# A decoder kernel: the first iteration of fp8 attention placed beside the last two state space iterations

## The chip, the cores and the metric

The kernel runs on one core of a Trainium2 chip. The metric is the device time of one execution in microseconds (us), the median of several runs. The core has five engines with a queue each, worked off in order: TensorE (PE) multiplies matrices, VectorE (DVE) and ScalarE (ACT) do elementwise work, GpSimd (POOL) does a share of it, and SyncE (SP) issues the DMAs. Engines wait for each other through semaphores. Matmul results land in PSUM, which has eight banks; all other data lies in SBUF.

## The reference

Six layers run one after another over 16 sequences of 128 tokens with 256 channels, each followed by a residual sum and a layer norm: linear attention, cross attention, a ternary MLP, a state space layer, fp8 attention, and a ternary linear layer. The change touches the fourth and the fifth. Cut to what matters:

```python
# layer 4: state space (per sequence)
zxbcdt = x @ W_in.T
xBC = silu(causal_conv(xBC, conv_w))
dt = softplus(dt_raw + dt_bias)
M = CB * Lmat * dtc[:, :, None, :, :]
Yd = jnp.einsum('bcijh,bcjhp->bcihp', M, xs_c)
yz = (Yd + D * xs) * silu(z)
return (yz * rsqrt(mean(yz * yz) + EPS) * norm_w) @ W_out.T

# layer 5: fp8 attention, self and cross, 32 query heads and 8 key/value heads each
ln_out = _ln(hidden_states, ln_w, ln_b)
q = _ln(_fp8_linear_pertensor(ln_out, wq, ...)); k, v, qx likewise
core = _gqa(q, k, v)
kx, vx = jnp.split(jnp.einsum('bsi,oi->bso', cond, w_kv_x), 2, axis=-1)
xout = _gqa(qx, _ln(kx, ...), vx)
catq = _div_clamp_fp8(jnp.concatenate([core, xout], axis=-1), proj_smooth)
return jnp.einsum('bsi,oi->bso', catq, wproj) * (proj_in_scale * proj_w_scale)
```

## The kernel before

One sequence (128 tokens on the 128 partitions) is one iteration of every stage. The stages follow each other; in each, the five engines have their own list of instructions, written out by hand in a function per engine (`sync`, `gpsimd`, `tensor`, `scalar`, `vector`), and the lists are worked off in order. A stage is pipelined in software: `steps(m, side, attend, front, back, ...)` is one iteration's worth of an engine's list, in which `front` prepares sequence m + 1, `attend` works on sequence m and `back` ends sequence m - 1.

**State space** (`state_space`, from line 1156). `sequences` calls `steps` for m = 0 to 17. In `attend`, the decay matrix is worked off in seven levels: TensorE multiplies `cb` and `xd` of a level into one of two banks `pL` (line 1404), VectorE scales the result by `dec` into `term` (1618), and GpSimd adds `term` to `y` (1350). Of the next sequence, `front` makes the projections and convolutions (banks `pZ`, `pX`, `pC`, `pE`), `xdt` and `xd`. In `back`, `y` is gated by `sz` (1625), transposed (1424), multiplied with `w_out` (1433), summed with `X` (1664) and normed; `vector_apply` (112) writes it back to `X`. m = 16 has `attend` and `back`, m = 17 only `back`. Beside this, m = 0 to 14 prepare the fp8 weights in `fa.w_all`.

**fp8 attention** (`fp8_attention_and_linear`, from line 1693). Each `steps` has eight units j = 0 to 7, one per four query heads. In `front`, unit j makes one block of four heads of keys or values of the next sequence, in the order k0, k1, v0, v1, k2, k3, v2, v3 (`OTHERS`; k0, k1, v0, v1 from the context `ctxT`, line 1910; the others from the quantised input, 1890). A key or query block is projected by TensorE into `pJB` or `pJA`, squared by ScalarE (2031), its `rs` made by GpSimd (1843, 1846), scaled by VectorE (`kn` 2174, `qn` 2180), transposed by TensorE into `pH` (1973, 2012) and copied by ScalarE (`kT`, `qT`, 2038); value blocks are only copied (`v`, 2076). The input is normed (`xn`, 2130), transposed (1999), copied (`lnT`, 2067) and quantised into four streams `xq` by VectorE and GpSimd (`stream_input`, 2139 to 2150; 1866; 2230). The first iteration, m = 0, has only `front`: units 0 to 7, and with them units 5 to 7 start queries 0 to 2 of sequence 1 (`there(j + 3)` and so on). Text calls it the head.

**Projection weights.** In the head SyncE loads `fa_wproj` in eight pieces of 512 KB into two buffers `wp_raw`, which lie in `cat`; a piece c from the third on waits until piece c - 2 is done (`wp_low`). ScalarE copies a piece to bf16 (2080, counted by `wp_high`), VectorE subtracts the copy (2234, counted by `wp_low`); both lie in `w_proj`, in the region shared with weights of the state space stage. Unit j treats piece j.

**The handover.** Every engine's list of the attention stage begins with `left` of the state space stage: a wait until `X` of the last sequence is written (`norm.x_done`), then one for `fa_ready`. After it come the iterations m = 0, 1, 2, 3, a hardware loop, and the last three. The eight PSUM banks of both stages are the same ones in turn, and their SBUF tensors overlap.

## Time and profile before

| | us |
|---|---|
| median of 3 runs | 2179.44 (2178.09 to 2184.95) |
| profiled execution | 2178.37 |
| its span, first to last instruction | 2176.6 |
| busy of the span: PE, DVE, ACT, POOL | 2028.2, 1624.8, 1333.5, 1274.6 |
| mean granted TensorE clock | 0.982 |

The span is what the profile shows from the first to the last instruction. The granted clock is the share of TensorE's full rate that the chip allowed: 1.00 is 2.4 GHz, 0.50 is 1.2 GHz. The state space stage ends at 1276.6 us of the span, where `X` of the last sequence is written; the head of the attention stage reaches to some 1330 us.

### The profile page before, as it was taken

How to read it: one execution, taken by the hardware profiler on the slowest of the kernel's cores; microseconds unless marked ns; L12 is line 12 of the kernel's file. 1: busy time of each engine (PE TensorE's matmuls, PEld its weight loads, DVE VectorE, ACT ScalarE, POOL GpSimd, SP SyncE). 2: the span in 40 equal slices, each digit the busy share in tenths (PEclk: the TensorE clock that was granted, in tenths of full speed). 3: DMA queues.
4: the chain of work that ended last, by engine and by line, in shares of the span. 5: the costliest groups of instructions: out<-in, count | busy, mean ns of one | idle time of the engine just before them, and what ended most of it. 6: DMA issues, size and time to landing. Idle time of an engine off the chain costs nothing.

```text
span 2176.6 us, 35701 instructions
## 1 busy us (share of the span) xinstructions
PE 2028.2 (93%) x10116; PEld 1329.1 (61%) x10116; DVE 1624.8 (75%) x3833; ACT 1333.5 (61%) x5022; POOL 1274.6 (59%) x1550
## 2 busy tenths in 40 slices
PE   7879999999999998899999957999999999999995
PEld 5636666666666665555655524666666666666664
DVE  7845667677776777787888746788888888788886
ACT  3555666666666665333343326777777777777773
POOL 0154454455444542578876734777777777777774
PEclk9999999999999999999999979999999999999998
DMA  6000000000000003000000011000000000000000
GB/s 225 1 18 6 3 4 3 2 5 2 2 2 2 2 1 141 9 20 20 20 20 10 1 47 40 4 4 6 6 6 5 6 5 6 8 5 6 3 3 8
DMA packets 30094, 37.62 MB, mean 17 GB/s; under 512 B 3328, under 2 KB 24320, under 8 KB 29312
## 3 DMA queue, kind: packets, MB, share of 16 engines
q1 hardware_dynamic: 29952, 36.11, 5.0%
q8 instruction: 42, 0.69, 0.1%
q14 instruction: 100, 0.82, 0.1%
HBM read 34.00 MB, written 2.10 MB: 17 GB/s over the span
## 4 chain that ended last, share of the span: by engine, by line
PE 63%; DVE 15%; ACT 11%; issue 7%; POOL 3%; DMA 0%; DVEq 0%; SPq 0%; POOLq 0%; ACTq 0%
PE xa_pS L755 5%; PE xa_pJB L736 5%; PE xa_pO L830 5%; PE xa_pY L867 5%; PE fa_pJB L1910 5%; PE xa_pJA L736 4%; PE ssm_pX L1410 4%; PE fa_pS L1929 3%; PE fa_pY L1962 3%; PE fa_pO L1949 3%; PE fa_pJA L1890 2%; PE ssm_pL L1404 2%; PE fa_pH L2012 2%; PE xa_pP L747 2%; POOL fa_rs L1846 2%
## 5 line engine op out<-in xcount | busy, mean ns | idle before, releaser
L2038 ACT ACTIVATE fa_qT<-fa_pH,all_fa_head_vec 128x512 f32<-128x512 f32 x128 | 99.6, 778 | 177.9 <-PE fa_pH L2012 177.9
L1846 POOL TENSOR_TENSOR fa_rs<-fa_rs,all_minus_half 128x4 f32<-128x4 f32 x192 | 197.9, 1031 | 15.0
L1350 POOL TENSOR_TENSOR ssm_y<-ssm_y,ssm_term 128x512 f32<-128x512 f32 x112 | 142.2, 1270 | 81.5 <-DVE ssm_term L1618 57.1
L2047 ACT ACTIVATE fa_pS<-fa_pS,fa_nb 128x128 f32<-128x128 f32 x512 | 183.3, 394 | 6.0 <-issue 6.0
L1843 POOL TENSOR_TENSOR fa_rs<-fa_ms,all_eps5w 128x4 f32<-128x4 f32 x192 | 44.4, 232 | 226.8 <-ACT fa_q_junk L2031 126.4
L1929 PEld LDWEIGHTS fa_pS<-fa_kT,fa_qT 128*128 128x128 f32 x1024 | 124.1, 191 | 65.2 <-ACT fa_qT L2038 58.4
L1871 POOL TENSOR_TENSOR fa_cat<-fa_ov,fa_om 128x512 bf16<-128x512 f32 x128 | 154.0, 1203 | 5.3
L1929 PE MATMUL fa_pS<-fa_kT,fa_qT 128*128 128x128 f32 x1024 | 148.1, 288 | 2.6 <-ACT fa_qT L2038 0.9
L1862 POOL TENSOR_TENSOR fa_ov<-fa_ob,fa_om 128x512 f32<-128x512 bf16 x128 | 148.0, 1157 | 3.2 <-DVE fa_om L2225 3.2
L682 POOL TENSOR_TENSOR xa_rs<-xa_ms,all_eps 128x4 f32<-128x4 f32 (+1 forms) x65 | 13.2, 203 | 222.6 <-ACT xa_junk L906 222.6
L924 ACT ACTIVATE xa_pr<-xa_pS,xa_nb,xa_rs 128x256 f32<-128x256 f32 x256 | 142.5, 568 | 0.2
L2180 DVE TENSOR_TENSOR fa_qn<-fa_pJA,fa_rs 128x512 f32<-128x512 f32 x128 | 88.4, 690 | 69.0 <-POOL fa_rs L1846 68.9
L1962 PE MATMUL fa_pY<-all_shared_weights,fa_cat 128*128 128x256 bf16 x1024 | 133.6, 274 | 4.8 <-POOL fa_cat L1871 4.8
L2031 ACT ACTIVATE fa_q_junk<-fa_pJA 128x128 bf16<-128x128 f32 x512 | 136.4, 302 | 0.4
L2047 ACT ACTIVATION_READ_ACCUMULATOR fa_pS<-fa_pS,fa_nb 128x1 f32 x512 | 134.0, 262 | 0.0
L1890 PE MATMUL fa_pJA<-fa_w_all,fa_xq 128*128 128x512 bf16 x512 | 133.0, 383 | 0.0
L1949 PE MATMUL fa_pO<-fa_pT,fa_v 128*128 128x256 f32 x512 | 131.9, 380 | 1.1 <-DVE fa_ob L2208 1.0
L1910 PE MATMUL fa_pJB<-all_shared_weights,fa_ctxT 128*128 128x512 f32 x256 | 126.2, 617 | 5.6 <-DMA fa_ctxT<-in_ctxT 4.9
L755 PE MATMUL xa_pS<-all_shared_weights,xa_qT 128*128 128x256 f32 x512 | 126.4, 387 | 5.3 <-ACT xa_qT L931 5.2
L1410 PE MATMUL ssm_pX<-ssm_w_tap,ssm_xT 128*128 128x512 f32 x256 | 122.6, 592 | 0.0
L867 PE MATMUL xa_pY<-xa_wo,xa_oT 128*128 128x256 f32 x512 | 121.4, 380 | 1.0 <-ACT xa_oT L952 1.0
L736 PE MATMUL xa_pJA<-all_shared_weights,xa_xT 128*128 128x512 f32 x256 | 121.5, 597 | 0.4 <-DVE xa_t L987 0.2
(330 smaller groups left out, 5844.7 us busy)
## 6 DMA issues: line engine op xcount, KB each, us to landing
all_shared_weights<-in_fa_w SPq DMA_DIRECT2D x12, 512.0 KB, 3.8
fa_cat<-in_fa_wproj SPq DMA_DIRECT2D x8, 512.0 KB, 3.8
all_shared_weights<-in_xa_wq SPq DMA_DIRECT2D x1, 2048.0 KB, 13.8
xa_wo<-in_xa_wo SPq DMA_DIRECT2D x1, 2048.0 KB, 17.2
xa_ctxT<-in_ctxT SPq DMA_DIRECT2D x16, 128.0 KB, 2.1
all_shared_weights<-in_fa_wkvx SPq DMA_DIRECT2D x1, 2048.0 KB, 10.0
fa_ctxT<-in_ctxT SPq DMA_DIRECT2D x16, 128.0 KB, 2.1
out_x<-all_X SPq DMA_DIRECT2D x16, 128.0 KB, 1.7
```

Of the source, the lines that this page charges most:

```text
L736: last = pe.matmul(bank[:, :], lhs[k], w[:, k, at0:at0 + 512], start=(k == 0), stop=(k == KT - 1))
L755: last = pe.matmul(pS[b][:, (h % 2) * NK:(h % 2 + 1) * NK], qT[:, n % 2, h, :], kT[:, to, :, n, :], start=True, stop=True)
L867: last = pe.matmul(pY[:, 0:D], oT[:, h, :], w_o[:, h, :], start=(h == 0), stop=(h == G * HG - 1))
L1410: return pe.matmul(pX[:, :], xT[:, k, t:t + P], w_tap[:, t, k, 0:HID], start=(n == 0), stop=(n == TAPS * KT - 1))
L1846: pool.tensor_tensor(rs[:, j % 2, cols], rs[:, j % 2, cols], env.mhalf[:, cols], ALU.pow)\
L1871: pool.tensor_tensor(cat[:, 4 * ((j - 3) % UNITS):4 * ((j - 3) % UNITS) + 4, :], ov[:, i], om[:, i], ALU.subtract).then_inc(a["cat"], 1)
L1890: last = pe.matmul(bank[:, :], xq[:, side, st, k, :], w_all[:, part, k, cols], start=(i == 0), stop=(i == 2 * KT - 1))
L1910: last = pe.matmul(pJB[:, :], ctxT[:, side, k, :], w_kvx[:, k, c * 512:(c + 1) * 512], start=(k == 0), stop=(k == KT - 1))
L1929: last = pe.matmul(pS[n % 2][:, i * P:(i + 1) * P], qT[:, n % 2, i, :], kT[:, to, 1 if n < 4 else 0, (4 * (n % 4) + i) // 2, :], start=Tru ...
L1949: last = pe.matmul(pO[:, 2 * i * P:(2 * i + 2) * P], v[:, to, 1 if n < 4 else 0, g * HD:(g + 1) * HD], pT[:, n % 2, 2 * i:2 * i + 2, :], s ...
L1962: last = pe.matmul(pY[:, 0:D], cat[:, hd, :], w_proj[:, part, hd, :], start=(n == 0 and i == 0), stop=(n == UNITS - 1 and i == 2 * HG - 1))
L2047: last = act.activation(four(pS[j % 2])[:, i, :], four(pS[j % 2])[:, i, :], ACT.Exp, bias=nb[:, j % 2, i:i + 1], accum_out=rsum[:, j % 2, ...
```

## The change

The function `sequences` of the attention stage no longer contains m = 0. Each engine's function of that stage returns two functions, `head` and `rest`. `head(j)` is unit j of m = 0; `head(0)` waits first for `ssm_front_left` and `fa_ready`. The state space stage calls it: units 0 to 3 inside m = 16, unit 4 inside m = 17, units 5 to 7 at the end of m = 17. On GpSimd, ScalarE and VectorE units 5 to 7 stand behind the wait (or the write) of the last `x_done`. `rest()` waits for `left` and runs the iterations from m = 1 on. `ssm_front_left` waits until what the state space stage's `front` reads and writes is done for the last time, and for the last level of m = 15.

So that this can be: `xd`, `cb`, `kT` and `v` become two tensors each (one per side), the SBUF tensors are allocated in another order, and so are the attention stage's banks. SyncE loads the first two context blocks behind `front_left` and the projection weights behind `left`. The pieces of the projection weights are treated by `PROJ_AT`: none in units 0 to 4, pieces 0 and 1 in unit 5, 2 to 4 in unit 6, 5 to 7 in unit 7. On VectorE the `vector_apply` of m = 17 for sequence 15 comes ahead of unit 4.

The diff, without the calls that only pass `head` on and the renamings of `xd`, `cb`, `kT` and `v` inside instructions:

```diff
+    for u in (1, 0):
+        xd[u], cb[u] = sb(f"xd{u}", [P, LEVELS, HID]), sb(f"cb{u}", [P, LEVELS, P])
-    xd = sb("xd", [P, 2, LEVELS, HID])
-    cb = sb("cb", [P, 2, LEVELS, P])
...
(state space, gpsimd)
                     if l == 6 and back:
                         norm.pool_rstd(pool, m - 1, 0)
+                    if m == B and l in (1, 2, 3, 5):
+                        head((1, 2, 3, 5).index(l))
             elif back:
                 pool_rms(m - 1)
+                head(4)
                 norm.pool_rstd(pool, m - 1, 0)
+                left(pool)
+                for j in (5, 6, 7):
+                    head(j)
...
(state space, tensor)
             next_level()
             next_level()
+            if m == B:
+                head(0)
             if back:
                 transpose_gated(m - 1)
+            if m == B + 1:
+                head(4)
...
                 if n in (0, 2, 4, 5, 6):
                     next_level()
+                if m == B and n in (0, 2, 5):
+                    head((0, 2, 5).index(n) + 1)
                 if back and n == 4:
                     project_out(m - 1)
...
             if first:
                 tail(1, 0)
+            if m == B + 1:
+                for j in (5, 6, 7):
+                    head(j)
...
(state space, scalar)
             if back and not front:
                 gated_out(m - 1)
+            if m == B:
+                for j in range(4):
+                    head(j)
+            if m == B + 1:
+                head(4)
+                left(act)
+                for j in (5, 6, 7):
+                    head(j)
...
(state space, vector)
+            if m == B:
+                head(0)
             if front:
                 softplus(m + 1)
...
             terms(2)
+            if m == B:
+                head(1)
             chunk_mean(m - 1)
             terms(3)
+            if m == B:
+                head(2)
+            if m == B + 1:
+                norm.vector_apply(dve, m - 2, 0)
+                head(4)
...
-            if m > 2:
+            if 2 < m <= B:
                 norm.vector_apply(dve, m - 2, 0)
             terms(4, 5)
...
                 norm.vector_stats(dve, m - 1, 0)
+            if m == B:
+                head(3)
             terms(6)
...
             if m == B + 1:
                 norm.vector_apply(dve, m - 1, 0)
+                for j in (5, 6, 7):
+                    head(j)
...
+    def front_left(eng):
+
+        for n in ("xs_ps", "bc_ps", "z_in", "xs_in", "cb_done", "cbd_done", "xdt_done", "dec_in"):
+            eng.wait_ge(s[n], now(B, 0))
+        eng.wait_ge(level_ps, now(B - 1, 0, LEVELS, LEVELS - 1))
...
(fp8 attention)
+    PROJ_AT = ((), (), (), (), (), (0, 1), (2, 3, 4), (5, 6, 7))
...
-    pJA, pJB = ps("pJA"), ps("pJB")
+    pJB, pH, pP, pJA = ps("pJB"), ps("pH"), ps("pP"), ps("pJA")
     pS = [ps("pS0"), ps("pS1")]
-    pH, pP, pO, pY = ps("pH"), ps("pP"), ps("pO"), ps("pY")
+    pY, pO = ps("pY"), ps("pO")
...
-        steps(0, 0, False, True, False, False)
         steps(1, 1, True, True, False, False)
...
+    def head_and_rest(eng, steps):
+
+
+        def head(j):
+            if j == 0:
+                env.ssm_front_left(eng)
+                eng.wait_ge(env.fa_ready, 1)
+            steps(0, 0, False, True, False, False, (j,))
+
+        def rest():
+            env.ssm_stage.left(eng)
+            sequences(eng, steps)
+        return head, rest
...
+        env.ssm_front_left(sp)
+        load(1, 1)
+        load(2, 0)
         env.ssm_stage.left(sp)
-        load(1, 1)
         load_proj(0)
         load_proj(1)
-        load(2, 0)
         for c in range(2, UNITS):
             sp.wait_ge(wp_low, c - 1)
             load_proj(c)
...
-                if not attend and front:
-                    act.wait_ge(wp_in[j % 2], 16 * (j // 2 + 1))
-                    act.activation(w_proj[:, 0, 4 * j:4 * j + 4, :], wp_raw[:, j % 2], ACT.Copy)\
+                for c in PROJ_AT[j] if not attend and front else ():
+                    act.wait_ge(wp_in[c % 2], 16 * (c // 2 + 1))
+                    act.activation(w_proj[:, 0, 4 * c:4 * c + 4, :], wp_raw[:, c % 2], ACT.Copy)\
                         .then_inc(wp_high, 1)
...
-                if not attend and front:
-                    dve.wait_ge(wp_high, j + 1)
-                    dve.tensor_tensor(w_proj[:, 1, 4 * j:4 * j + 4, :], wp_raw[:, j % 2],
-                                      w_proj[:, 0, 4 * j:4 * j + 4, :], ALU.subtract).then_inc(wp_low, 1)
+                for c in PROJ_AT[j] if not attend and front else ():
+                    dve.wait_ge(wp_high, c + 1)
+                    dve.tensor_tensor(w_proj[:, 1, 4 * c:4 * c + 4, :], wp_raw[:, c % 2],
+                                      w_proj[:, 0, 4 * c:4 * c + 4, :], ALU.subtract).then_inc(wp_low, 1)
...
                 @block.tensor
                 def _(pe):
                     env.la.tensor(pe)
                     tail = env.xa_stage.tensor(pe)
-                    env.ssm_stage.tensor(pe, tail)
-                    env.fa_stage.tensor(pe)
+                    head, rest = env.fa_stage.tensor(pe)
+                    env.ssm_stage.tensor(pe, tail, head)
+                    rest()
```

## Rows read from the trace of the kernel before

**Rows 1.** Stretches: length, busy by engine (PE, PEld, DVE, ACT, POOL), clock, DMA, GB/s.

```profile
1248.00:1270.00 22.00, 12.79 (x45) 6.93 (x43) 13.44 (x19) 3.67 (x7) 18.35 (x16) 0.92 0.00 0
1270.00:1279.00 9.00, 3.50 (x8) 2.54 (x9) 2.54 (x10) 1.17 (x3) 1.84 (x4) 0.71 0.08 20
1279.00:1300.00 21.00, 11.81 (x22) 5.33 (x22) 5.06 (x9) 6.43 (x22) 3.10 (x5) 0.58 0.33 105
...
1345.00:1400.00 55.00, 54.02 (x324) 37.34 (x323) 42.65 (x105) 42.42 (x200) 37.05 (x46) 1.00 0.01 3
```

**Rows 2.** The chain that ended last, in order of time: start, us, what.

```profile
1241.47 1.73 PE ssm_pO L1433 x8
...
1244.05 0.86 PE ssm_pL L1404 x2
...
1250.29 0.55 ACT ssm_dec L1548
...
1259.73 1.27 POOL ssm_y L1350
...
1266.39 0.70 DVE ssm_term L1618
...
1270.61 3.52 PE ssm_pO L1433 x8
...
1287.21 1.12 PE fa_pH L1973 x4
1288.32 2.99 PE fa_pJB L1910 x4
...
1314.37 0.95 ACT all_shared_weights L2080
...
1329.89 1.02 POOL fa_rs L1846
```

**Rows 3.** Timeline of VectorE, the state space end and one piece of the weights.

```profile
1253.15 1.56 DVE L1625 TENSOR_TENSOR ssm_y<-ssm_y,ssm_sz 128x512 f32<-128x512 f32 x1
...
1268.52 0.69 DVE L1625 TENSOR_TENSOR ssm_y<-ssm_y,ssm_sz 128x512 f32<-128x512 f32 x1 [1.44 <-POOL ssm_y L1350]
...
1274.15 0.48 DVE L1664 SCALAR_TENSOR_TENSOR ssm_res<-ssm_pO,ssm_rms,all_X 128x256 f32<-128x256 f32 x1 [4.61 <-PE ssm_pO L1433]
...
1276.22 0.41 DVE L112 TENSOR_SCALAR all_X<-ssm_res,ssm_mean_var,ssm_rstd 128x256 f32<-128x256 f32 x1 [0.66 <-POOL ssm_rstd L107]
...
1315.35 1.23 DVE L2234 TENSOR_TENSOR all_shared_weights<-fa_cat,all_shared_weights 128x1024 bf16<-128x1024 f32 x1 [3.52 <-ACT all_shared_weights L2080]
```

**Rows 4.** Timeline of ScalarE in the head.

```profile
1300.83 0.60 ACT L2076 ACTIVATE fa_v<-fa_pJB 128x512 f32<-128x512 f32 x1 [2.63 <-PE fa_pJB L1910]
...
1322.29 0.27 ACT L2031 ACTIVATE fa_q_junk<-fa_pJA 128x128 bf16<-128x128 f32 x1
...
1328.39 0.28 ACT L2031 ACTIVATE fa_q_junk<-fa_pJA 128x128 bf16<-128x128 f32 x1
...
1332.38 0.78 ACT L2038 ACTIVATE fa_qT<-fa_pH,all_fa_head_vec 128x512 f32<-128x512 f32 x1 [1.45 <-PE fa_pH L2012]
```

**Rows 5.** Timeline of TensorE; in brackets idle time before and what ended it.

```profile
1253.33 3.59 PE L1404 MATMUL ssm_pL<-ssm_xd,ssm_cb 128*128 128x512 f32 x4 [3.48 <-issue]
...
1279.01 3.75 PE L1910 MATMUL fa_pJB<-all_shared_weights,fa_ctxT 128*128 128x512 f32 x4 [4.90 <-DMA fa_ctxT<-in_ctxT]
...
1296.27 1.11 PE L1973 MATMUL fa_pH<-all_ident,fa_kn 128*128 128x128 f32 x4 [4.74 <-DVE fa_kn L2174]
...
1310.37 1.12 PE L1973 MATMUL fa_pH<-all_ident,fa_kn 128*128 128x128 f32 x4 [4.04 <-DVE fa_kn L2174]
```

**Rows 6.** A short stretch, TensorE alone: length, busy, granted clock, DMA share, GB/s.

```profile
1257.00:1258.00 1.00, 1.00 (x6) 1.00 0.00 0
```

**Rows 7.** By source line: landing of the weights; VectorE's stream multiplication, ns min/median/max.

```profile
DMA to landing us min/median/max: 3.6/3.8/5.2
...
L2139 DVE TENSOR_TENSOR fa_xv<-fa_lnT,all_fa_inv_scale x64: 413/583/1199, 1296.1 to 2096.1; 128x256 f32<-128x256 f32 x64
```

More of the change, by code:

```diff
@@ L1333, in sync, with gpsimd @@
                 .then_inc(raw_in[n % RAWS], 16)
-    def gpsimd(pool, tail):
+    def gpsimd(pool, tail, head):
         def pool_rms(b):
@@ L1385, in gpsimd, with tensor @@
         sequences(pool, steps)
-    def tensor(pe, tail):
+    def tensor(pe, tail, head):
         def transpose_x(b):
@@ L1496, in tensor, with scalar @@
         sequences(pe, steps)
-    def scalar(act, tail):
+    def scalar(act, tail, head):
         def chunk_high(n):
@@ L1554, in scalar, with vector @@
         sequences(act, steps)
-    def vector(dve, tail):
+    def vector(dve, tail, head):
         def softplus(m):
@@ L1847, in rstd, with steps @@
                 .then_inc(sems["rstd"], 1)
-        def steps(m, side, attend, front, back, last_linear):
+        def steps(m, side, attend, front, back, last_linear, js=range(UNITS)):
             there = presence(attend, front, back)
-            for j in range(UNITS):
+            for j in js:
                 if front and j > 0 and OTHERS[j - 1][0] == "k":
@@ L1878, in steps @@
                     norm.pool_rstd(pool, m - 1, 0)
-        env.ssm_stage.left(pool)
-        pool.wait_ge(env.fa_ready, 1)
-        sequences(pool, steps)
+        return head_and_rest(pool, steps)
     def tensor(pe):
@@ L1916, in other, with steps @@
             last.then_inc(kk["ps"] if kind == "k" else v_ps, 1)
-        def steps(m, side, attend, front, back, last_linear):
+        def steps(m, side, attend, front, back, last_linear, js=range(UNITS)):
             there = presence(attend, front, back)
-            for j in range(UNITS):
+            for j in js:
                 keys = front and j > 0 and OTHERS[j - 1][0] == "k"
@@ L2021, in steps @@
                     project(pJA, to, Q8 if n < 4 else QX8, n % 4).then_inc(q["ps"], 1)
[L2023 to L2025 removed]
+        return head_and_rest(pe, steps)
     def scalar(act):
@@ L2039, in head_in, with steps @@
                            scale=head_vec[:, c:c + 1]).then_inc(sems["T_in"], 1)
-        def steps(m, side, attend, front, back, last_linear):
+        def steps(m, side, attend, front, back, last_linear, js=range(UNITS)):
             there = presence(attend, front, back)
-            for j in range(UNITS):
+            for j in js:
                 if there(j):
@@ L2151, in stream_input, with steps @@
                     .then_inc(sx["xm_done"], 1)
-        def steps(m, side, attend, front, back, last_linear):
+        def steps(m, side, attend, front, back, last_linear, js=range(UNITS)):
             there = presence(attend, front, back)
-            for j in range(UNITS):
+            for j in js:
                 if back and j == 4:
@@ L2337, in _ @@
                     tail = env.xa_stage.gpsimd(pool)
-                    env.ssm_stage.gpsimd(pool, tail)
-                    env.fa_stage.gpsimd(pool)
+                    head, rest = env.fa_stage.gpsimd(pool)
+                    env.ssm_stage.gpsimd(pool, tail, head)
+                    rest()
                 @block.tensor
@@ L2351, in _ @@
                     tail = env.xa_stage.scalar(act)
-                    env.ssm_stage.scalar(act, tail)
-                    env.fa_stage.scalar(act)
+                    head, rest = env.fa_stage.scalar(act)
+                    env.ssm_stage.scalar(act, tail, head)
+                    rest()
                 @block.vector
@@ L2358, in _ @@
                     tail = env.xa_stage.vector(dve)
-                    env.ssm_stage.vector(dve, tail)
-                    env.fa_stage.vector(dve)
+                    head, rest = env.fa_stage.vector(dve)
+                    env.ssm_stage.vector(dve, tail, head)
+                    rest()
 def constants():
```

53 lines of the change are left out of this document (25 added, 28 removed).

## The prediction, made before the changed kernel ran

> **What bounds the kernel now.** TensorE is busy for 2028.2 of 2176.6 us (the table), so I first looked for where it is not. The table of stretches [rows 1] has the answer: at 1345 to 1400 us, in the attention loop, TensorE is busy 54.02 of 55 us; from 1248 to 1300 us it is busy 12.79 + 3.50 + 11.81 = 28.1 of 52 us. That hole is the place of the change: the last two state space iterations (m = 16 and 17) and the first attention iteration (its m = 0, a "head" of eight units j). Outside it nothing is touched, so only two questions matter: when does the first full attention iteration start, and does it run as before after that. I then read the engines' timelines and the chain that ended last, from 1250 us on. The reader is to see two chains of small links, each with one engine at work. In the state space end a level goes TensorE, VectorE (`term`), GpSimd (`y` += `term`), 0.86, 0.7 and 1.27 us [rows 2]; the last output is applied at 1276.22 + 0.41 = 1276.6 us [rows 3]. In the head a unit goes ScalarE squares, GpSimd `rs`, VectorE scaling, TensorE transposes. The last squares of the head begin at 1328.39 us and its last query is copied at 1332.38 us [rows 4]; this copy is my finishing line. Everything behind it is the same code in the same order.
>
> **The clock.** TensorE's granted clock is at 0.50 (1.2 GHz) in many of these short bursts. It idled before 1253.33 us (3.48 us), 1279.01 (4.90), 1296.27 (4.74) and 1310.37 (4.04) [rows 5], and the bursts behind them took about twice as long as such bursts at full clock; behind the first the clock was back at 1257 us [rows 6]. I take the lower level for some 3.5 to 4.5 us after each such gap, by using the measured length of the like burst.
>
> **What the change moves.** Units 0 to 3 of the head go into m = 16, unit 4 into m = 17, and 5 to 7 behind it; queues are in order, so each head step on an engine now stands ahead of the rest of the state space iteration. I add up the new order link by link.
>
> Until 1256.8 us nothing differs: levels 0 and 1 still wait for `xd` and run 1253.33 to 1256.9 [rows 5]. The condition for the head (`dec_in`, at 1250.83 [rows 2]) has passed, and the context block is asked for then and takes less than the 4.9 us that TensorE waits for it at 1279.01 [rows 5]: hidden, it is there before 1256.8, and that wait is gone.
>
> Unit 0 (key block 0) goes ahead of the transposes of `y`: 4 matmuls, 1.7 us at full clock. Level 2 is issued at 1258.9 and read at 1260.0, 0.25 us late. GpSimd: adds 0 and 1 end at 1261.0 [rows 2], rms 0.8, `rs0` 0.55, add 2 1.27, then `rs` of key block 0 1.3 (1.02 [rows 2] and the sum before it), to 1264.9; VectorE scales it (0.7), TensorE starts unit 1 at 1265.6. **It has idled 5.8 us there, with level 3 queued behind.** Unit 1 is two groups of transposes and a projection, 1.12 + 2.99 = 4.1 us at the lower clock as from 1287.21 us [rows 2], to 1269.8; level 3 0.86, `term` 0.7, add 3 1.27, `rs` of block 1 1.3, scaling 0.7: TensorE starts unit 2 at 1274.9, again after a gap over 4 us. Transposes and value block take 4.56 us, as 1296.27 to 1300.83 [rows 4, 5], to 1279.4. Level 4, output projection and level 5 follow at full clock, 0.86 + 1.73 + 0.86 [rows 2], to 1282.9. VectorE: `term` 0.7, sum and statistics 1.3, four stream steps 1.3, `xq` 0.4, `term` 6 0.7, to 1287.2. For one cost the trace has only neighbours: stream steps of VectorE beside GpSimd's adds. Of the multiplication they begin with the trace has 413 ns at least, 583 in the median and 1199 at most [rows 7]; I take +0.5 us, with 0 and +2 as ends, as one group of four meets GpSimd at work on the path. So 1287.7; add 6 1.27, gating 0.7 [rows 2, 3], TensorE at 1289.7. There the transposes (0.45), unit 4's projection (1.9 at the lower clock) and the output projection (2.7, between 1.73 and 3.52 [rows 2]) end at 1294.8, and sum, statistics and apply take 2.5 us as from 1274.15 to 1276.63 [rows 3]. **The last state space output comes at 1297.3 us, 20.7 us later than now.** Units 0 to 4 are then done, so unit 5 starts on TensorE at 1299.4 instead of 1310.37 [rows 5]: a gain of 10.9 us so far.
>
> A rule of the Trainium skill bears on the same neighbours. VectorE's gating took 1.56 us beside GpSimd at work and 0.69 us alone [rows 3]. By the Trainium skill, "SBUF — State Buffer", section "Who interferes with whom", a VectorE instruction with two SBUF inputs waits for the whole of a GpSimd instruction that reads SBUF, and the reverse. The rows agree with that; by it the group could lose up to a whole add more, some 1 us for my 0.5.
>
> **What gives the gain back.** The projection weights. Now one of their 8 pieces is loaded, copied (ScalarE) and subtracted (VectorE) in each unit; SyncE starts at 1276.6, with the state space stage left. After the change SyncE still waits for that output, now at 1297.3, and no piece has been done by unit 5, where 4 have been done so far. `PROJ_AT` puts pieces 0 and 1 in unit 5, 2 to 4 in unit 6, 5 to 7 in unit 7, all ahead of the unit's query squares on ScalarE. There are two raw buffers, so piece c can be asked for only when c - 2 is subtracted: landing 3.8 us (3.6 to 5.2, [rows 7]), copy 0.95 to the next instruction, subtraction 1.23 [rows 2, 3].
>
> Unit 5: squares of key block 2 shifted by -10.9; both pieces have landed at 1302.2, before ScalarE comes to them at 1303.3; one piece more than now on ScalarE costs 0.95, and one more on VectorE makes key block 3's scaling late, so unit 6 comes on TensorE with a shift of -9.8. Unit 6: ScalarE is at piece 2 at 1311.6, which has landed; 2 and 3 cost 1.9; piece 2 is subtracted at 1313.9, piece 4 lands at 1317.7, and **ScalarE waits 4.1 us for it**, with the squares of query 1 behind. They start at 1318.6 where now it is 1322.29 [rows 4], so -3.7 is left. Their `rs`, scaling, and transposes at the lower clock (TensorE has idled since 1313.7, +0.45) set unit 7. Unit 7: value copy, pieces 5 and 6; piece 5 is subtracted at 1326.4, piece 7 lands at 1330.2, **ScalarE waits 4.1 us again**, copies, and begins query 2's squares at 1331.1, against 1328.39: +2.7. Transposes at the lower clock once more, +0.4. At the finishing line +3.1 us.
>
> Checked by the pieces: -10.9 gained, +1.1 in unit 5 (one more copy ahead of the squares, and VectorE's queue), +3.8 for two more copies each in units 6 and 7, +8.2 for the two waits, +0.9 for twice the low clock: +3.1.
>
> Edits at nothing: `xd`, `cb`, `kT` and `v` split and buffers in a new order (same instructions); the bank order (they free one by one); the earlier `vector_apply` of m = 15 (waits for `rstd` that GpSimd has 0.5 us after add 6, while VectorE is gating; uncovered it would be 0.5); waits in `front_left` (passed when reached); `wp_low` in m = 1, unit 3 (piece 7 is done by 1333 us, unit 3 comes near 1350).
>
> The profiled execution took 2178.37 us for a span of 2176.6; the runs' median is 2179.44. 2178.4 + 3.1 = **2181.5 us**, 0.1% above the median. A measurement of this kernel can tell about 0.3% (6.5 us) from no change.
>
> **The rivals.**
>
> **B.** The weights ride along. If pieces 4 and 7 were there when ScalarE comes to them, 8.2 us fewer stand in the sum: 2173.3, and with the two low clocks gone too 2172.4, which is just faster. For it: SyncE and the queues are idle, and landing took 3.6 at best. Against: piece 4 waits for piece 2's subtraction by the two buffers, and only piece 3's copy (0.95) lies between; no landing in the trace is that short. And an earlier state space end would not shrink the waits. 0.08.
>
> **C.** Slower: TensorE keeps the lower clock through m = 16. The two new gaps (5.8 and over 4 us) follow one another with some 5 us of work between. If the clock does not come back between 1265.6 and the end of the output projection, level 3, level 4, projection and level 5 double (0.86 + 0.86 + 1.73 + 0.86 = 4.3), value block 1 and level 6 (2.6) end after VectorE is ready for them and add about 1.1, and the last output projection 0.8: +6.2, together 2187.7. It decides from +3.4 us on, that is from half of it. For it: from 1279 to 1300 us bursts like these often ran at the lower level [rows 5, 6]. Against: behind the second gap TensorE has over 10 us of unbroken work, and the clock came back after 3.5 us at 1257. 0.17.
>
> **D.** The overlap does not come about: something in `front_left` is late and holds the head back until the state space end. Then units 0 to 3 lose the weight pieces (about 6 us shorter), but the whole of the two waits stays: the last output at 1276.6, units 0 to 4 in 33.8 - 6 = 27.8, and from unit 5 to the end of query 2's squares 32.8 as above: 1337.2 against 1329.4, so 2178.4 + 7.8 = 2186.2. Against: all eight counts are reached by 1251 us by the timelines. 0.03.
>
> **How the numbers follow.** Forecast with its width 0.72, B 0.08, C 0.17, D 0.03. Bounds of the unknown costs: landing 3.6 to 5.2 twice (-0.4 to +2.8), VectorE beside GpSimd -0.5 to +1.5, clock per gap +-1 over five gaps. For 8 in 10: 2175 to 2189, which leaves out half of B, D and the far end of C. Faster by over 0.3% (under 2172.9): half of B and little else, 0.08. Slower by over 0.3% (over 2186.0): C, D and a tail of the forecast, 0.2. The same: 0.72.
>
> **What the profile of the changed kernel would show.** In m = 16, TensorE idles over 5 us ahead of key block 0's transposes and over 4 us ahead of block 1's, each ended by VectorE's `kn`, and then runs at the lower clock. The last `all_X` of the state space stage comes near 1297 us. The first piece of `fa_wproj` is issued right behind it. ScalarE idles about 4 us ahead of its fifth and eighth copy of the weights, ended by a DMA, and the copies come in groups of 2, 3 and 3. The span from 1345 us on is as before, moved by some 3 us. I would be wrong if the last state space output came before 1290 us, if those two waits were short, or if the m = 1 iteration took another length than now.

## The result: slightly slower, inside the range, and the profile after

The changed kernel takes **2185.93 us** (median of 10 runs, 2182.34 to 2187.15), the kernel before 2180.07 us (10 runs, 2177.14 to 2184.95). The ratio is **1.0024**, 95% interval 1.0015 to 1.0032: slower by 5.2 us, which is under 0.3%. The forecast was 2181.5 us, 3.1 us above the profiled execution of before. The profiled execution took 2184.38 us for a span of 2182.6 us, 6.0 more than before.

The stretches, with the columns of [rows 1]:

```profile
1248.00:1270.00 22.00, 12.85 (x38) 6.55 (x37) 9.96 (x13) 5.44 (x15) 14.65 (x14) 0.78 0.04 12
1270.00:1279.00 9.00, 4.82 (x12) 2.56 (x11) 2.78 (x7) 2.61 (x11) 2.44 (x3) 0.69 0.00 0
1279.00:1300.00 21.00, 12.58 (x36) 6.93 (x34) 9.56 (x27) 3.54 (x13) 8.61 (x12) 0.83 0.01 2
...
1320.00:1345.00 25.00, 14.42 (x51) 9.54 (x52) 11.89 (x20) 13.67 (x57) 5.41 (x9) 0.69 0.16 50
1345.00:1400.00 55.00, 53.18 (x324) 37.09 (x321) 38.98 (x95) 43.16 (x208) 35.76 (x46) 1.00 0.01 4
```

In the first three stretches TensorE does 30.3 us of work instead of 28.1 [rows 1], at a granted clock of 0.78, 0.69 and 0.83 (before 0.92, 0.71 and 0.58). In the first two, part of the head's work is there now (ScalarE 8.1 us instead of 4.8), and yet the stretch from 1320 to 1345 us is thin: 14.42 us of TensorE's work at 0.69. In the kernel before, the same stretch has more of TensorE's, ScalarE's and GpSimd's work, as m = 1 has already begun in it:

```profile
1320.00:1345.00 25.00, 18.29 (x97) 11.24 (x96) 11.53 (x21) 18.91 (x86) 7.76 (x13) 0.97 0.01 3
```

TensorE's timeline shows where it idles (brackets: idle time before, and what ended it):

```profile
1253.45 3.65 PE L1411 MATMUL ssm_pL<-ssm_xd,ssm_cb 128*128 128x512 f32 x4 [3.48 <-issue]
...
1265.79 1.11 PE L2031 MATMUL fa_pH<-all_ident,fa_kn 128*128 128x128 f32 x4 [5.67 <-DVE fa_kn L2228]
...
1275.77 1.11 PE L2031 MATMUL fa_pH<-all_ident,fa_kn 128*128 128x128 f32 x4 [4.18 <-DVE fa_kn L2228]
...
1290.82 0.92 PE L1431 MATMUL ssm_pY<-all_ident,ssm_y 128*128 128x128 f32 x4 [4.17 <-DVE ssm_y L1649]
...
1300.43 1.12 PE L2031 MATMUL fa_pH<-all_ident,fa_kn 128*128 128x128 f32 x4 [4.68 <-DVE fa_kn L2228]
...
1308.43 1.12 PE L2031 MATMUL fa_pH<-all_ident,fa_kn 128*128 128x128 f32 x4 [3.52 <-DVE fa_kn L2228]
...
1323.57 1.12 PE L2070 MATMUL fa_pH<-all_ident,fa_qn 128*128 128x128 f32 x4 [8.79 <-DVE fa_qn L2234]
...
1336.30 1.11 PE L2070 MATMUL fa_pH<-all_ident,fa_qn 128*128 128x128 f32 x4 [6.16 <-DVE fa_qn L2234]
1337.20 1.91 PE L1948 MATMUL fa_pJA<-fa_w_all,fa_xq 128*128 128x512 bf16 x4
```

Four matmuls of transposes take 0.6 to 0.7 us at full clock; in these lines they take 0.92 to 1.12. Every idle time but the first is ended by VectorE (a scaling or the gating of `y`), the end of a chain of small links. The two longest, 8.79 and 6.16 us, stand ahead of queries 1 and 2. ScalarE's timeline says what lies behind those two:

```profile
1304.31 2.01 ACT L2136 ACTIVATE all_shared_weights<-fa_cat 128x1024 bf16<-128x1024 f32 x2
...
1313.09 2.00 ACT L2136 ACTIVATE all_shared_weights<-fa_cat 128x1024 bf16<-128x1024 f32 x2
1319.33 1.06 ACT L2136 ACTIVATE all_shared_weights<-fa_cat 128x1024 bf16<-128x1024 f32 x1 [4.24 <-DMA fa_cat<-in_fa_wproj]
1320.29 0.26 ACT L2087 ACTIVATE fa_q_junk<-fa_pJA 128x128 bf16<-128x128 f32 x1
...
1325.88 2.00 ACT L2136 ACTIVATE all_shared_weights<-fa_cat 128x1024 bf16<-128x1024 f32 x2
...
1332.00 1.06 ACT L2136 ACTIVATE all_shared_weights<-fa_cat 128x1024 bf16<-128x1024 f32 x1 [4.12 <-DMA fa_cat<-in_fa_wproj]
1332.96 0.26 ACT L2087 ACTIVATE fa_q_junk<-fa_pJA 128x128 bf16<-128x128 f32 x1
...
1337.45 0.78 ACT L2094 ACTIVATE fa_qT<-fa_pH,all_fa_head_vec 128x512 f32<-128x512 f32 x1 [1.97 <-PE fa_pH L2070]
```

The copies of the weights come in groups of 2, 3 and 3. In the two groups of three ScalarE waits 4.24 and 4.12 us for the last piece, with a query's squares right behind. The chain that ended last runs through exactly these loads (start, us, what):

```profile
1314.18 1.24 DVE all_shared_weights L2288
1315.43 3.88 DMA fa_cat<-in_fa_wproj
1319.33 1.06 ACT all_shared_weights L2136
...
1326.97 1.24 DVE all_shared_weights L2288
1328.22 3.76 DMA fa_cat<-in_fa_wproj
```

A subtraction frees the buffer, a load fills it, ScalarE copies. In the kernel before, no load stood on this chain between 1285 and 1345 us.

### The profile page after: what moved, and what is told of

The parts are those of the page before. It is cut to its first block, busy times and chain, and to the rows that moved or that the text cites. A ratio compares the mean times of both kernels' runs of the same rounds, so it can differ in the third digit from the quotient of the medians.

```text
span 2182.6 us, 35726 instructions
## 1 busy us (share of the span) xinstructions
PE 2031.7 (93%) x10116; PEld 1333.2 (61%) x10116; DVE 1623.8 (74%) x3833; ACT 1332.0 (61%) x5022; POOL 1272.2 (58%) x1550
## 4 chain that ended last, share of the span: by engine, by line
PE 63%; DVE 15%; ACT 11%; issue 7%; POOL 4%; DMA 1%; DVEq 0%; SPq 0%; POOLq 0%; ACTq 0%
PE xa_pS L755 5%; PE xa_pJB L736 5%; PE xa_pO L830 5%; PE xa_pY L867 5%; PE fa_pJB L1968 5%; PE xa_pJA L736 4%; PE ssm_pX L1417 4%; PE fa_pS L1987 3%; PE ssm_pL L1411 3%; PE fa_pJA L1948 3%; PE fa_pY L2020 3%; PE fa_pO L2007 2%; PE fa_pH L2070 2%; PE xa_pP L747 2%; POOL fa_rs L1906 2%
## 5 line engine op out<-in xcount | busy, mean ns | idle before, releaser
L1903 POOL TENSOR_TENSOR fa_rs<-fa_ms,all_eps5w 128x4 f32<-128x4 f32 x192 | 44.3, 231 | 228.0 <-ACT fa_q_junk L2087 141.2
L2218 DVE TENSOR_REDUCE fa_nb<-fa_pS 128x4 f32<-128x512 f32 x128 | 87.8, 686 | 46.8 <-PE fa_pS L1987 32.6
```

## The experiments

The interval of a ratio can't say where a microsecond went, so each run is also read by three landmarks of its profile, and only their differences are compared: **L** is the start of level 0 of m = 16 on TensorE, **X** the start of the last `all_X` of the state space stage, **S** the start of VectorE's statistics of `X` in unit 0 of m = 1, where the loop's work begins. Nothing ahead of L is edited, but for fillers in e7. In the changed kernel X and S are:

```profile
1297.87 0.41 DVE L112 TENSOR_SCALAR all_X<-ssm_res,ssm_mean_var,ssm_rstd 128x256 f32<-128x256 f32 x1 [0.67 <-POOL ssm_rstd L107]
...
1336.97 0.42 DVE L2176 BATCH_NORM_STATS2 fa_st<-all_X 128x6 f32<-128x256 f32 x1
```

The landmarks are those of one execution each. Where nothing was edited between L and X, the stretch still came out 0.9 us longer in e8 than in the kernel before and 1.1 us shorter in e9 than in the changed kernel, so a difference of a microsecond between two rows is not told by them. A ratio is against runs of the kernel before on the same chip; their median was 2180.25 us for e1 to e4, 2183.27 for e5 to e8, 2180.31 for e9 and e10.

| kernel | L to X | X to S | L to S | against before | ratio, 95% interval |
|---|---|---|---|---|---|
| before | 22.9 | 56.1 | 79.0 | | |
| changed | 44.4 | 39.1 | 83.5 | +4.5 | 1.0024 (1.0015 to 1.0032) |
| e1, no landing waits | 44.2 | 31.2 | 75.4 | -3.6 | 0.9984 (0.9975 to 0.9994) |
| e2, grouped alone | 23.0 | 69.5 | 92.5 | +13.5 | 1.0065 (1.0048 to 1.0081) |
| e3, fillers in the state space part | 38.4 | 39.4 | 77.8 | -1.2 | 0.9999 (0.999 to 1.0009) |
| e4, levels first | 37.3 | 39.2 | 76.6 | -2.4 | 0.9986 (0.9977 to 0.9996) |
| e5, pieces early | 44.3 | 24.7 | 69.0 | -10.0 | 0.9947 (0.993 to 0.9964) |
| e6, e5 and e4 | 37.9 | 24.0 | 61.9 | -17.1 | 0.9924 (0.9908 to 0.9941) |
| e7, e6 and fillers | 33.9 | 24.4 | 58.3 | -20.7 | 0.9892 (0.9872 to 0.9912) |
| e8, before with fillers | 23.8 | 53.4 | 77.2 | -1.8 | 0.9981 (0.9971 to 0.9991) |
| e9, changed, fillers behind X | 43.3 | 36.6 | 79.9 | +0.9 | 1.0004 (0.9994 to 1.0014) |
| e10, before, other fillers | 22.8 | 51.2 | 74.0 | -5.0 | 0.9981 (0.9972 to 0.9991) |

The handover differences and the timed ratios tell the same to within 3 us (1.0024 of 2180 is +5.2 beside +4.5, 0.9892 is -23.6 beside -20.7), so most of what a run changes in the time is changed between L and S. A little lies behind S: in the changed kernel from there to the end of the span it is another 1.4 us (845.6 beside 844.2). The rivals after the result were three: the waits for the weights, the longer state space end, and the low clock.

**e1: the two waits.** It leaves out six of the eight loads and makes all eight pieces from the first two; it only prices the waits. Against the changed kernel:

```diff
-        for c in range(2, UNITS):
-            sp.wait_ge(wp_low, c - 1)
-            load_proj(c)
...
-                    act.wait_ge(wp_in[c % 2], 16 * (c // 2 + 1))
+                    act.wait_ge(wp_in[c % 2], 16)
```

> The changed kernel, but only weight pieces 0 and 1 are loaded; ScalarE and VectorE make all eight pieces from these two buffers, so no copy waits for a DMA behind a subtraction (this leaves out six of the eight loads, and the weights made from them). The copies and subtractions themselves stay. Theory W (the two waits of 4.24 and 4.12 us for landings stand on the path to the first full attention iteration): ScalarE's squares of query 1 and 2 begin 4.2 and 8.4 us earlier, TensorE's gaps of 8.8 and 6.2 us become 4.5 and 2, the clock comes back in part, and the time falls by 8 to 10 us, to 2176 to 2178 us. Rival K (the clock is what gives the gain back, the waits only overlap with it): less than 4 us.

Measured: 2176.01 us. X stays where it was (44.2 us after L); from X to S 31.2 us instead of 39.1, so the waits cost **7.9 us** of the handover. TensorE's idle times ahead of queries 1 and 2 fell from 8.79 and 6.16 us to:

```profile
1320.82 1.12 PE L2067 MATMUL fa_pH<-all_ident,fa_qn 128*128 128x128 f32 x4 [4.81 <-DVE fa_qn L2231]
...
1329.63 0.99 PE L2067 MATMUL fa_pH<-all_ident,fa_qn 128*128 128x128 f32 x4 [1.98 <-DVE fa_qn L2231]
```

3.98 + 4.18 = 8.2 us. The two waits together are 8.36 us: nearly all of it was on the path.

**e2: the grouping without the move.** The kernel before, with only `PROJ_AT` of the change:

```diff
+    PROJ_AT = ((), (), (), (), (), (0, 1), (2, 3, 4), (5, 6, 7))
...
-                if not attend and front:
-                    act.wait_ge(wp_in[j % 2], 16 * (j // 2 + 1))
+                for c in PROJ_AT[j] if not attend and front else ():
+                    act.wait_ge(wp_in[c % 2], 16 * (c // 2 + 1))
```

> The kernel before, with the weight pieces grouped as in the change (none in units 0 to 4, then 2, 3 and 3), and nothing else of it: the head stays behind the state space stage. Theory W: units 0 to 4 get about 6 us shorter, units 5 to 7 carry five more copies and two waits of 4 us each; +7.8 us with the sum of the prediction, with the clock at its lower level behind the long gaps some +8 to +11, so 2188 to 2191 us. Rival K: the grouping alone costs under 3 us.

Measured: 2193.2 us, +13.5 us in the handover, more than expected. The same waits are there:

```profile
1328.34 1.06 ACT L2081 ACTIVATE all_shared_weights<-fa_cat 128x1024 bf16<-128x1024 f32 x1 [4.03 <-DMA fa_cat<-in_fa_wproj]
...
1341.19 1.06 ACT L2081 ACTIVATE all_shared_weights<-fa_cat 128x1024 bf16<-128x1024 f32 x1 [4.29 <-DMA fa_cat<-in_fa_wproj]
```

So the grouping costs 13.5 us by itself. If grouping and move simply add, which no run shows, the move brings 4.5 - 13.5 = -9.0. Most of what made my expectation too small is on record: unit 5's key transposes come 55.9 us after L (1309.44) where it was 57.0 in the kernel before, so leaving the pieces out of units 0 to 4 gave back 1.2 us, not the 6 that I had counted.

**e3: the low clock in m = 16 and 17.** Matmuls of nothing needed (`warm`), ahead of unit 1, unit 2 and the last transposes of `y`, so that TensorE doesn't idle long:

```diff
+        def warm(n):
+            for _ in range(n):
+                pe.matmul(pE[:, :], fa.w_all[:, 0, 0, 0:P], fa.w_all[:, 0, 0, 0:512], start=True, stop=True)
...
+            if m == B + 1:
+                warm(13)
             if back:
                 transpose_gated(m - 1)
...
                 if m == B and n in (0, 2, 5):
+                    warm({0: 20, 2: 13, 5: 0}[n])
                     head((0, 2, 5).index(n) + 1)
```

> The changed kernel with extra bf16 matmuls of 512 columns into an unused bank while TensorE would idle ahead of unit 1 (20), unit 2 (13) and the last transposes of y (13); nothing reads them. They take 4.3, 2.8 and 2.8 us at full clock. Theory K: the bursts behind these gaps were on the path at half rate: unit 1 4.75 us falls to 2.9, unit 2 4.3 to 2.4, level 4 by 0.4, transposes, projection and output projection by 1.5; the last state space output comes 4 to 5.5 us earlier than 1298.3 and the time falls by as much, to 2181 us. Rival: the clock is not granted for them, or the bursts are not on the path: no change, or some us slower where the matmuls delay the real ones.

Measured: X comes 38.4 us after L instead of 44.4, and behind X nothing changes (39.4 beside 39.1). TensorE:

```profile
1261.42 4.26 PE L1404 MATMUL ssm_pE<-fa_w_all 128*128 128x512 bf16 x19
...
1267.05 0.66 PE L2038 MATMUL fa_pH<-all_ident,fa_kn 128*128 128x128 f32 x4 [1.37 <-DVE fa_kn L2235]
```

The filler takes 0.22 us a matmul, the idle time is 1.37 us instead of 5.67, and the transposes take 0.66 us instead of 1.11. So behind the three gaps that the fillers close the low clock cost **6.0 us** ahead of X in the changed kernel, a little more than the 4 to 5.5 expected; the timed median, 2179.9 us, is 6.0 lower as well.

**e4: the state space steps first.** The head's units stand further back, so that the waits for `kn` come when the levels that are ready have been issued:

```diff
(tensor)
-                if n in (0, 2, 4, 5, 6):
+                for _ in range({0: 2, 2: 2, 4: 1}.get(n, 0) if m == B else n in (0, 2, 4, 5, 6)):
                     next_level()
...
(vector)
-            if m == B:
-                head(1)
             chunk_mean(m - 1)
             terms(3)
             if m == B:
+                head(1)
+                terms(4, 5)
                 head(2)
...
(gpsimd)
-                    if m == B and l in (1, 2, 3, 5):
-                        head((1, 2, 3, 5).index(l))
+                    if m == B and l in (1, 2, 3, 6):
+                        head((1, 2, 3, 6).index(l))
```

> The changed kernel with another order in m = 16: TensorE does levels 2 and 3 ahead of unit 1, levels 4 and 5 ahead of unit 2, level 6 and the output projection ahead of unit 3; VectorE and GpSimd follow (GpSimd's unit 3 behind add 6). Theory S (the state space end slips by 21 us mainly since its levels are queued behind TensorE's waits for the head): the last state space output comes 4 to 6 us earlier, near 1293 us, and the time falls by as much, to 2180 to 2182 us. Rival: the slip comes from the head's own chain, which then ends no earlier: within 1 us of the changed kernel.

Measured: 2176.82 us; X at 37.3 us after L, 7.1 earlier than in the changed kernel, and unchanged behind it (39.2). The idle times of 4.18 and 4.17 us became:

```profile
1275.88 0.67 PE L2032 MATMUL fa_pH<-all_ident,fa_kn 128*128 128x128 f32 x4 [2.32 <-DVE fa_kn L2229]
...
1284.86 0.71 PE L1431 MATMUL ssm_pY<-all_ident,ssm_y 128*128 128x128 f32 x4 [2.29 <-DVE ssm_y L1649]
```

The transposes themselves ran at full clock in both. Behind the second it fell again at once: three matmuls of unit 4's projection took 1.49 us, at a granted clock of 0.50. The 7.1 us are 1 more than the 6 at most that I expected, and the time is 9.1 us under the changed kernel. Part of it is order and part is clock; the run does not tell how much of each.

**e5: the pieces into the free time of m = 16 and 17.** Six of the eight are loaded behind `front_left` into space that is free then (`kT[0][:, 0]`, and 4 KB behind the shared weights), and treated in units 0 to 5; the last two into the old buffers behind `left`, one in unit 6, one in unit 7, both there long before:

```diff
-    PROJ_AT = ((), (), (), (), (), (0, 1), (2, 3, 4), (5, 6, 7))
+    PIECES = (0, 1, 2, 6, 7, 5, 3, 4)
+    HIGH_AT = ((0, 1), (2, 3), (), (4,), (), (5,), (6,), (7,))
+    LOW_AT = ((), (0, 1), (2, 3), (), (4,), (5,), (6,), (7,))
...
+    raws = (first_raw, second_raw, first_raw, second_raw, first_raw, first_raw, wp_raw[:, 0], wp_raw[:, 1])
...
-        env.ssm_stage.left(sp)
         load_proj(0)
         load_proj(1)
-        for c in range(2, UNITS):
-            sp.wait_ge(wp_low, c - 1)
-            load_proj(c)
+        for i, done in ((2, 1), (3, 2), (4, 3), (5, 5)):
+            sp.wait_ge(wp_low, done)
+            load_proj(i)
+        env.ssm_stage.left(sp)
+        load_proj(6)
+        load_proj(7)
```

> The changed kernel, with the head and the state space stage in its order, but five of the eight weight pieces (0, 1, 2, 6, 7, whose places in the shared region are free by then) are loaded right behind the condition for the head into two buffers that are free then, copied and subtracted where ScalarE and VectorE idle in m = 16 and 17; the other three are treated one in each of units 5, 6 and 7, loaded before ScalarE comes to them. Theory W: the state space end stays at 45 us behind level 0, from unit 5 on all goes as in the kernel before, 9.9 us earlier than there; so 2170 to 2171 us, 15 us under the changed kernel. Rival: the early pieces get in the way of the chain in m = 16 (last output later by more than 2 us) or DMA landings are late again: 2175 us or more.

Measured: **2170.54 us, 0.53% faster than before** and 14.5 us shorter in the handover than the changed kernel. Five pieces in m = 16 and 17 cost nothing there (L to X 44.3 beside 44.4), and X to S fell by 14.4 us. The copies no longer wait, and TensorE's idle times ahead of queries 1 and 2 are 2.14 and 1.74 us, with full clock behind:

```profile
1314.43 0.66 PE L2078 MATMUL fa_pH<-all_ident,fa_qn 128*128 128x128 f32 x4 [2.14 <-DVE fa_qn L2250]
...
1320.59 0.65 PE L2078 MATMUL fa_pH<-all_ident,fa_qn 128*128 128x128 f32 x4 [1.74 <-DVE fa_qn L2250]
```

Of the 14.4 us, 7.9 are e1's waits. I put the other 6.5 down to two copies fewer ahead of each query's squares and to the full clock; no run takes these apart.

**e6 and e7: the pieces together.** e6 is e5 with the edit of e4; e7 adds `warm` of e3 with other counts (9 ahead of level 0, 15 ahead of unit 1, 5 ahead of unit 2, 5 ahead of the last transposes of `y`) and 14 ahead of unit 5:

```diff
+            if m == B:
+                pe.wait_ge(s["dec_in"], now(B, 0))
+                warm(9)
...
+                    warm({0: 15, 2: 5, 5: 0}[n])
...
+                warm(14)
                 for j in (5, 6, 7):
                     head(j)
```

> The early pieces together with the order of the levels of the run before last (levels 2 and 3 ahead of unit 1, 4 and 5 ahead of unit 2). If slip and waits are two independent terms, their gains add: 15 us for the pieces and 7 to 9 us for the levels, so 2162 to 2164 us. Rival: with the state space end earlier the weights become late once more, and the sum is less, 2166 us or more.

> The same, with extra bf16 matmuls that nothing reads in TensorE's gaps: 9 ahead of level 0 in m = 16, 15 ahead of unit 1, 5 ahead of unit 2 and of the last transposes of y, 14 ahead of unit 5. Theory K as a third, smaller term: levels 0 and 1 3.6 us falls to 1.9 (GpSimd's xd ends only at 1256.2, so about 1 us of it counts), unit 1 1.9 us shorter, unit 5 1.8 us; 3 to 5 us under the run without them. Rival: nothing, as other engines end last there.

Measured: 2164.89 and **2157.63 us**. For e6 that is 0.9 above the range expected and below its rival's 2166. In the handover e5 is 14.5 us better than the changed kernel, e4 7.0, and e6 has 21.6: the two add up. They act on different sides of X (24.0 behind it in e6, 24.7 in e5; 37.9 ahead of it, 37.3 in e4). e7 has 3.6 us more: 4.0 ahead of X, and 0.4 are lost behind it, so the fillers ahead of unit 5 gave nothing that the landmarks show. The timed medians differ by 7.3 us, but e6 and e7 have four runs each, which spread over 5.3 and 7.0 us. e7 is **1.08% faster than the kernel before** (0.9892, 0.9872 to 0.9912). In the stretches from 1300 to 1345 us of the changed kernel and of e7:

```profile
1300.00:1345.00 45.00, 25.25 (x91) 15.24 (x92) 20.06 (x33) 23.11 (x81) 8.96 (x15) 0.72 0.30 96
```

```profile
1300.00:1345.00 45.00, 37.90 (x214) 25.11 (x217) 29.70 (x70) 33.96 (x162) 22.36 (x31) 1.00 0.02 4
```

In e7 m = 1 begins at 1310.75 us and fills most of this stretch; in the changed kernel it begins at 1336.97. So TensorE does 214 matmuls in the time of 91, at a clock of 1.00 instead of 0.72.

**e8 and e10: is the low clock the change's?** The kernel before with fillers in its head: e8 has them ahead of units 0, 1, 2 and 5 (15 ahead of unit 0), e10 the same without those ahead of unit 0:

```diff
+                if front and not attend:
+                    for _ in range({1: 13, 2: 14, 5: 12}.get(j, 0)):
+                        pe.matmul(pJA[:, :], w_all[:, 0, 0, 0:P], w_all[:, 0, 0, 0:512], start=True, stop=True)
```

> The kernel before, with extra bf16 matmuls that nothing reads in TensorE's gaps ahead of unit 0 (15), 1 (13), 2 (14) and 5 (12). Theory K holds for any order of this handover: unit 0's projection 3.75 us falls to 1.9, unit 1 4.1 to 2.4, unit 2 4.5 to 2.6, unit 5 by 1.5: 5 to 7 us less, 2173 to 2175 us. If the low clock were a burden of the change only, the kernel before would stay within 1 us.

> The kernel before, with the extra matmuls of the last such run but for those ahead of unit 0, which themselves ran at half rate there and took 5.4 us, so that unit 0 began 6.3 us later. Ahead of unit 1 13, unit 2 14, unit 5 12. From unit 0's start to the statistics of m = 1 it was 53.3 us in the kernel before and 47.1 with all of them, 1.9 of that in unit 0's projection: so 4 to 5 us less than the kernel before. Rival: without them unit 1's are at half rate too and delay it, no gain.

Measured: 2179.59 and 2175.63 us, both 0.9981 of their own runs of before. e8 missed its -5 to -7: the handover shrank by 1.8 us alone, or 2.7 if only X to S is taken (53.4 beside 56.1). Its fillers ahead of unit 0 stand behind an idle time and ran at the low clock themselves:

```profile
1279.83 5.59 PE L1924 MATMUL fa_pJA<-fa_w_all 128*128 128x512 bf16 x14 [2.99 <-DVE all_X L112]
```

0.4 us a matmul instead of 0.22, and unit 0 had to wait for them until 1285.26 us. Without them (e10) the handover is 5.0 us shorter, as expected. The timed ratios don't tell e8 from e10: two of e8's ten runs took 2173.8 and 2174.1 us, at a mean clock of 0.987 and 0.988, the others 2178.8 to 2181.3. So the low clock is no cost of the change alone: the kernel before paid some 4 to 5 us for it, by e10's ratio between 2.0 and 6.1.

**e9: the clock behind X.** The changed kernel with fillers ahead of units 5 and 6 and of the transposes of queries 1 and 2:

```diff
+                def warm(n):
+                    for _ in range(n):
+                        pe.matmul(pY[:, :], w_all[:, 0, 0, 0:P], w_all[:, 0, 0, 0:512], start=True, stop=True)
+                if front and not attend:
+                    warm({5: 14, 6: 9}.get(j, 0))
...
+                    if not back:
+                        warm(32 if not attend and j == 7 else 20 if attend and j == 0 else 0)
```

> The changed kernel, with extra bf16 matmuls that nothing reads in TensorE's gaps behind the state space stage only: 14 ahead of unit 5, 9 ahead of unit 6, 32 ahead of query 1's transposes and 20 ahead of query 2's. Theory: what the forecast missed (2181.5 against 2185.9) is the clock in these units and in m = 1, which the sum took at full rate or left out: unit 5 0.5 us and its projections 1.4, unit 6 1.0, queries 1 and 2 0.5 each, the first units of m = 1 1.1; the state space end stays at 44.4 us behind level 0, the start of m = 1 comes 3 to 5 us earlier, 2181 to 2183 us. Rival: the waits for landings absorb it, less than 1.5 us.

Measured: 2181.54 us, 1.0004: 4.4 us below the changed kernel (1.0004 against 1.0024), as expected. X to S is 36.6 us instead of 39.1, with the waits for the weights untouched (4.05 and 4.19 us); another 1.1 us lie ahead of X, where nothing was edited (below). TensorE at full clock behind query 1's fillers, and in the scores behind query 2's transposes, which took 1.91 us in the changed kernel:

```profile
1321.98 0.66 PE L2078 MATMUL fa_pH<-all_ident,fa_qn 128*128 128x128 f32 x4 [1.17 <-DVE fa_qn L2242]
...
1335.84 1.16 PE L1993 MATMUL fa_pS<-fa_kT,fa_qT 128*128 128x128 f32 x8
```

## Why the prediction was right, and where its sum was too small

In order, by the prediction's own steps. Absolute times of after lie 0.12 us late from level 0 on (1253.45 beside 1253.33), before the change touches anything.

- **The order and the new idle times: right.** Predicted 5.8 us ahead of unit 1 and over 4 ahead of unit 2, ended by VectorE's `kn`; measured 5.67 and 4.18. Unit 1 at 1265.6, measured 1265.79.
- **Unit 2 at 1274.9, measured 1275.77: short by 0.75.** I had 4.1 us for unit 1, from a neighbour; it took 4.75, as its projection ran 3.62 us and the transposes of `xn` behind it were slow too (0.62 beside 0.38). Level 3 was back at the full clock.
- **VectorE beside GpSimd, +0.5 us: right.** The four stream steps beside GpSimd took 1.66 us (from 1286.04) and 1.27 without it (from 1275.63): 0.4 more, nearly all in the second step, 0.64 us instead of 0.29, and not the whole add more that it could have been.
- **Last output at 1297.3, measured 1298.3 (its 0.41 us included): +1.0.** e3 says how much of the 44.4 us is clock: 6.0.
- **Unit 5 at 1299.4, measured 1300.43; unit 6 shifted by -9.8, measured -8.8** (1308.43 beside 1317.23): the same 1 us as at X, no further loss. But the idle time of 3.52 us ahead of unit 6 was followed by the low clock (1.12 us), which I had not counted there: query 0's transposes came 2.61 us behind the key transposes instead of 1.86, another 0.75.
- **The two waits, 4.1 us each: right** (4.24 and 4.12), as was their cause, two raw buffers and one copy between. e1 confirms that both are on the path. (The kernel before had done five pieces ahead of unit 5's key transposes, not four as I wrote; no term of the sum hangs on it.) Squares of query 1 at 1318.6, measured 1320.29; of query 2 at 1331.1, measured 1332.96.
- **The finishing line, +3.1, measured +5.07** (1337.45 beside 1332.38). The 1.97 us more are the 0.12 of the start, some 0.9 from the clock ahead of X, 0.75 in unit 6 and 0.2 left over. The term that was too small is the clock's: I had it at +0.9 behind X, for two of the three idle times that are followed by the low clock here and were not before (ahead of unit 6 and of queries 1 and 2).
- **"The m = 1 iteration runs as before": wrong.** Its first key transposes come 6.2 us later than before, against 5.07 at the line. I had taken everything behind the line as the same code, but the same code at another clock is not the same time. In the kernel before TensorE had idled 1.69 us ahead of query 2's transposes, and the projection and scores behind them took 1.03 and 1.16 us. Here it had idled 6.16 us, and they took 1.91 us each. Two short stretches, TensorE alone (length, busy, clock, DMA share, GB/s):

```profile
1336.00:1339.00 3.00, 2.70 (x9) 0.50 0.01 3
1339.00:1342.00 3.00, 2.68 (x13) 0.50 0.00 0
```

That is the other 1.1 us. From there on all is 6.2 us late and stays so: the statistics of the next m come at 1387.82 beside 1381.65 us. From S to there m = 1 takes 50.9 us instead of 49.3, and another length of m = 1 was one of my own signs of being wrong.

So the term that was too small is the clock's, by some 1.7 us ahead of the finishing line and 1.1 behind it. e9 shows it from the other side: with fillers behind X alone X to S is 2.5 us shorter, and the ratio falls to no difference (another 1.1 us of its handover lie ahead of X, where nothing was edited).

The median lies 4.4 us above the forecast, and the clock is not all of that. Some 3 us are the terms above. The other 1.5 are the executions': the sum stood on one that took 2178.37 us, 1.7 below the median of the kernel before (2180.07), and the profiled one of the changed kernel lies as far below its own (2184.38 beside 2185.93). The larger misses all have the same sign, so none hid another; the forecast held since its range was wide, 2175 to 2189 us.

**The rivals.** B (the weights ride along) did not happen: both waits are there in full. Its price of 8.2 us was right, as e1 shows, and so was the reason, since only other buffers (e5) took them away. C (low clock all through m = 16) did not happen: behind unit 2 only level 4 was slow (1.39 us instead of 1.02), and the output projection and levels 5 and 6 took full-clock times:

```profile
1281.33 1.89 PE L1440 MATMUL ssm_pO<-all_shared_weights,ssm_yT 128*128 128x256 f32 x8
1283.05 1.02 PE L1411 MATMUL ssm_pL<-ssm_xd,ssm_cb 128*128 128x512 f32 x2
```

But it points to the term that was too small; e3 says that 6.0 us of the state space end are the clock's, of which my sum, 1 us short at X, had all but about one. D (no overlap) is refuted by X at 44.4 us after L and units 0 to 4 done by then. Its price was wrong too: it took units 0 to 3 as 6 us shorter without the pieces, and by e2 that is 1.2 us for units 0 to 4.

What the prediction did not ask was whether the weights had to be treated in groups at all. By e2 the grouping costs 13.5 us, so that by difference, not shown by itself, the overlap brings 9.0; with the pieces treated where ScalarE and VectorE have time for them (e5), the same overlap ends 10.0 us ahead of the kernel before.

## What to carry to other kernels

When the head of a stage is moved under the end of the one before, list what the old end still releases (here the place for the weights, through `left` and two raw buffers), since that is what the head waits for next; move its loads and their treatment too, to where the engines idle. In queues worked off in order, put a wait that may be long behind all the work that is ready: here two waits of 4 us ahead of the squares cost 8 us, and state space steps issued ahead of the head's waits gave 7 back, clock included. A moved stage is priced with TensorE's clock behind each new idle time, and "the same code behind" only where the idle time ahead of it stays the same too.

## What the runs showed of the hardware

The granted clock behind an idle time of the same length does not always fall at the same moment. Behind 4.18 us ahead of unit 2 the transposes took 1.11 us in the changed kernel and in e5 (1.12), but in e9, with the same instructions up to there:

```profile
1277.09 0.66 PE L2037 MATMUL fa_pH<-all_ident,fa_kn 128*128 128x128 f32 x4 [4.18 <-DVE fa_kn L2236]
```

Behind 4.69 us ahead of unit 5 they took 1.12 us in e5 and 0.66 in e6. In e9 and in e6 the clock fell right behind these transposes: to 0.59 in e9 (1277.6 to 1279.0 us), to 0.50 in e6 (1294.6 to 1298.0), where the projection took 1.86 us instead of 1.03:

```profile
1294.06 0.66 PE L2040 MATMUL fa_pH<-all_ident,fa_kn 128*128 128x128 f32 x4 [4.69 <-DVE fa_kn L2245]
1294.55 1.86 PE L1957 MATMUL fa_pJB<-fa_w_all,fa_xq 128*128 128x512 bf16 x4
```

Nor does the length alone decide. Behind 3.59 us ahead of query 2's transposes in e9 the clock stayed at 1.00 (1334 to 1338 us), while a shorter idle time ahead of unit 6 in e7 was followed by the low clock:

```profile
1294.81 1.11 PE L2051 MATMUL fa_pH<-all_ident,fa_kn 128*128 128x128 f32 x4 [2.33 <-DVE fa_kn L2256]
```

What decides was not found out. In e9 the later fall shortened the way from unit 2's key transposes to level 4 from 4.33 to 3.65 us. Such differences make up its unexpected 1.1 us ahead of X: L to unit 1's key transposes took 0.6 us more than in the changed kernel, from there to unit 2's 0.9 less, and from there to the last transposes of `y` 0.8 less.

The fillers that e8 started behind 2.99 us of idle time were slow themselves (0.40 us a matmul) and held up what they were to help; those that e3 started right behind other work ran at full clock (0.22 us).

VectorE's scaling of `xn` took 0.41 us in the kernel before and 1.34 in the changed one, where GpSimd adds a `term` to `y` beside it (1262.44 to 1263.70 us):

```profile
1262.51 1.34 DVE L2184 TENSOR_SCALAR fa_xn<-all_X,fa_mv,fa_rs 128x256 f32<-128x256 f32 x1 [1.66 <-POOL fa_rs L1935]
```

It was not on the path: the scaling of `kn` behind it waited another 1.19 us for GpSimd's `rs`.
